# Preparing causal attention inside the stages before it: a four-stage transformer kernel on one Trainium2 core

## The chip, the core and the metric

The kernel runs on one core of a Trainium2 chip. TensorE (PE) multiplies matrices, VectorE (DVE) and ScalarE (ACT) work element by element, GpSimd (POOL) does some adds and powers, and SyncE (SP) issues most DMA transfers. Each engine runs its own instructions in program order; semaphores order them against each other. The metric is the device time in microseconds (us) of one execution.

## The reference, cut to what matters

Two layers over 2 x 2048 tokens of 128 features; each sub-layer f is applied as `x = x + layernorm(f(layernorm(x)))`. The four sub-layers are local attention over segments of 64 tokens, an attention with a mixture of 8 experts and a shared one behind it, causal attention with 2 heads of width 128 and one shared key and value head, and a second, sparse mixture. The change lies in the second and the third:

```python
# second: the mixture; combine holds two non-zero weights a token
shared = _swiglu(xf, sW1, sW2, sW3)
h = silu(einsum('td,efd->etf', xf, eW1)) * einsum('td,efd->etf', xf, eW3)
moe_out = shared + einsum('te,etd->td', combine, einsum('etf,edf->etd', h, eW2))
# third: causal attention, here on layernorm(x)
k = apply_rope(x @ Wk.T); v = x @ Wv.T
q = apply_rope(einsum('btd,hkd->bhtk', x, Wq))
scores = where(causal, einsum('bhtk,bsk->bhts', q, k) * scale, -inf)
out = einsum('bhts,bsk->bhtk', softmax(scores), v).transpose(0, 2, 1, 3).reshape(B, T, 256) @ Wo.T
```

`layernorm` takes off the mean of each token's 128 features and divides by the root of variance plus 1e-5.

## The kernel before

X stays in SBUF as 32 tiles of 128 tokens x 128 features; four tiles are a block of 512 tokens. Products that need precision are split in a high and a low part and made in three matmuls (`matmul_split`, L64 to L66). An `nc.Block()` gives each engine its own list of work; at its end all engines meet.

**The mixture** (`ffn_mixture`, second block) runs over 72 items: 8 token blocks, each with the shared expert and 8 others. For item t TensorE makes the two up products (three items ahead of the down product), ACT the silu (L1624), VectorE the product with the gate side (`hidden`, L1662), GpSimd the expert's weight (L1647), ACT the high part (`high`, L1608), VectorE the low part (`low`, L1667), and TensorE the down product. When a token block's nine items are through, ACT copies the sum (`keep_down`, L1614), TensorE turns it, and `finish` on VectorE takes it in parts, one beside each of the following items, 15 items late (`FIN_LAG`): part 0 adds x2 (L1675), parts 1 to 4 take the statistics of one tile each (L1791, L1793), GpSimd makes the power at part 4 (L1812), parts 6 to 8 apply mean and scale to four tiles (L1683, `APPLY0`), and at part 8 GpSimd adds the result to X (L1639).

**Between** stands a block of its own at the head of `causal_attention`: SP loads the projection weights, the mask and the rotation table `cs` (2 MB, into `room`); VectorE takes the statistics of all 32 tiles in four chunks (L719 to L727), with GpSimd's powers (L738), then rotates the weights (L2051, L2052); ACT makes their high part (L2067), VectorE the low part (L2054). GpSimd zeroes two areas (L2652, L2763).

**Causal attention** runs over two batches. `load(b)` makes the 2048 tokens' keys, queries and values in four turns of 512: VectorE norms four tiles (`norm`, L2223; two turns ahead), TensorE turns them (L2459), ACT makes two copies (`copies`, L2391 and L2392), VectorE the low part (`low`, L2228), TensorE v (L2470) and three rotated projections. For each of the three, VectorE multiplies by `cs` (`rope`, L2235), GpSimd adds the two halves (L2352), ACT makes the high part (L2396), VectorE the low part (L2241). Then 16 rows of 128 queries follow: scores, maxima on VectorE (L2268), exponentials on ACT (L2421), transposes, copies of them on VectorE (L2332), values (L2529), the output copy on ACT (L2429) and `row_done` on VectorE. In batch 1 a function `between` puts work for the last stage beside the rows, among it rows' norms on ACT (L2784). GpSimd's list in a batch is the rotation adds and then one power for each four rows. SP's list holds the last stage's tables and the clearing of d_xs, 17 MB in DRAM.

Of the kernel before, what the change touches and what calls it, by code (L numbers as in the profile page):

```python
# [5 lines left out]
F32 = mybir.dt.float32  # L6
F32R = mybir.dt.float32r
# [6 lines left out]
P = 128  # L14
# [716 lines left out]

def stats_pool(nc, pool, S, rows=slice(0, 2), chunks=range(4)):
# [609 lines left out]
APPLY0 = {6: (0, 1), 7: (2,), 8: (3,)}  # L1342
# [4 lines left out]
def ffn_mixture(nc, dr, X, g, S, w, ao, x2):  # L1347

    m = Mem(nc, "b2_")
    with m:  # L1350
# [190 lines left out]
        F = FinishNorm(m, by_rows=True)  # L1541
        ub = m.ps("ub", 4)
# [35 lines left out]
        with nc.Block() as block:  # L1578
            @block.sync
            def _(sp):  # L1580
# [3 lines left out]

                keep_gates(0)
                for n in range(NBLK):
# [6 lines left out]
                    if n + 1 < NBLK:  # L1593
                        keep_gates(n + 1)

            @block.scalar
            def _(act):
# [21 lines left out]
                for t in range(ITEMS + KEEP_LAG):  # L1619
# [8 lines left out]
                    if k == 0 and n >= 1:  # L1628
                        keep_down(n - 1)
                    n, k = divmod(t, NX)  # L1630
                    if k == TURN_AT + UP_LAG and n + 1 < NBLK:
                        gate_rows(n + 1)

            @block.gpsimd
            def _(pool):
# [5 lines left out]
                for t in range(ITEMS + FIN_LAG):  # L1641
# [10 lines left out]
                    if k == ADD_PART and 0 <= n < NBLK:  # L1652
                        add_back(n)

            @block.vector
            def _(dve):
# [13 lines left out]
                def finish(n, part):  # L1670
# [16 lines left out]
                router.best(nc, dve, 1)  # L1687
                for t in range(ITEMS + FIN_LAG + NX):
# [207 lines left out]
def ffn_layer0(nc, dr, X, g):  # L1896
    with Mem(nc, "b_") as m:
# [12 lines left out]
        ffn_mixture(nc, dr, X, g, S, w, ao, x2)  # L1910
# [95 lines left out]
HC = 2  # L2006
SCALE_C = float(D) ** -0.5


FRONT_AT = 3  # L2010
SENDS = (14, 17)
def causal_attention(nc, dr, X, g, W, LF):
    with Mem(nc, "c_") as m:
        NW = 2 * (1 + HC)
        wh = m.sb("wh", [P, NW, D], F32R)
        wl = m.sb("wl", [P, NW, D], F32R)
        wv = m.sb("wv", [P, D])
        wo = m.sb("wo", [P, HC, D])
        mask = m.sb("mask", [P, P], BF16)
# [7 lines left out]
        with Mem(nc, "c0_") as t:  # L2027
            S = Stats(m, t, g)
            raw = t.sb("raw", [P, NW, D])
            w_in = t.sem("w_in")  # L2030
            c_in = t.sem("c_in")
            rot = t.sem("rot")
            hi = t.sem("hi")
            lo = t.sem("lo")
            with nc.Block() as block:
                @block.sync
                def _(sp):
                    sp.dma_start(raw[:, 0::2, :], dr["c_wkq"]).then_inc(w_in, 16)
                    for dst, src in ((wv[:, :], "c_wv"), (wo[:, :, :], "c_wo"), (mask[:, :], "mask1"),
                                     (cs[:, :, :, :], "cs1")):  # L2040
                        sp.dma_start(dst, dr[src]).then_inc(c_in, 16)
                    sp.wait_ge(c_in, 16 * 4)

                @block.vector
                def _(dve):
                    def weights():
                        dve.wait_ge(w_in, 16)
                        for k in range(0, NW, 2):
                            src = raw[:, k, :].rearrange("p (n two) -> p n two", two=2)
                            dst = raw[:, k + 1, :].rearrange("p (n two) -> p n two", two=2)  # L2050
# [1481 lines left out]
```

## Time and profile before

| | us |
|---|---|
| three runs, median (lowest to highest) | 2020.51 (2020.46 to 2022.98) |
| profiled execution | 2022.49 |
| its span | 2020.3 |
| PE, DVE, POOL, ACT busy of the span | 86%, 72%, 51%, 49% |

The span runs from the first instruction to the last; the execution's own time has about 2 us more around it. In a timeline row stand the start and the length in us, engine, line, operation, what is written and read, and the number of instructions merged (x4); in brackets how long the engine had been idle and what ended that. In the windows busy time is given for PE, PEld (weight loads), DVE, ACT and POOL in this order; a busy PE is not PE at its peak. The granted clock is a share of 2.4 GHz.

### The profile page before, as it was taken

The page shows a single profiled execution, that of the slowest core. Times are in us where ns is not written, and L with a number is a line of the kernel's source. Part 1 is how long each engine was busy: PE and PEld are TensorE (multiplying, and loading weights), DVE is VectorE, ACT ScalarE, POOL GpSimd, SP SyncE. Part 2 cuts the span into 40 slices and gives each one's busy share as a digit, 9 for nine tenths or more (in the row PEclk, how much of TensorE's full clock was granted, in tenths as well). Part 3 has the DMA queues.
Part 4 walks back from the last instruction along what each step waited for, and adds up shares of the span by engine and source line. Part 5 has one row for each costly group of instructions (what it writes and reads, how often), then busy time and mean ns, then how long its engine had stood idle before and what let it go on. Part 6 is the DMA issues. An engine that isn't in the chain of part 4 may idle for free. (4 is left out here: it accounts for less than half of the span.)

```text
span 2020.3 us, 37074 instructions
## 1 busy us (share of the span) xinstructions
PE 1730.4 (86%) x13636; PEld 1314.7 (65%) x13636; DVE 1456.8 (72%) x3406; ACT 984.5 (49%) x2221; POOL 1027.2 (51%) x684
## 2 busy tenths in 40 slices
PE   3899999998589999999998899947898689959993
PEld 2677877877445665666665776625786477748782
DVE  5688778778478877877884688877776777863234
ACT  2456555555315676556656455413332263326564
POOL 3466556556307896777865356642000400356554
PEclk9899999999759999999999899968999899979996
DMA  5212112111100000000000133349200000026663
GB/s 167 79 70 83 63 70 82 69 75 69 44 0 1 1 1 1 1 1 1 1 1 1 45 104 95 94 124 232 44 1 0 1 1 1 23 63 201 207 220 113
DMA packets 78467, 124.08 MB, mean 61 GB/s; under 512 B 11824, under 2 KB 43440, under 8 KB 77776
## 3 DMA queue, kind: packets, MB, share of 16 engines
q1 hardware_dynamic: 73744, 112.31, 18.3%
q0 software_dynamic: 4544, 9.41, 1.4%
q8 instruction: 109, 1.79, 0.4%
q14 instruction: 70, 0.57, 0.1%
HBM read 59.19 MB, written 28.94 MB: 44 GB/s over the span
## 5 line engine op out<-in xcount | busy, mean ns | idle before, releaser
L1088 ACT ACTIVATE mb_pt<-mb_stb 128x1024 f32<-128x1024 f32 x256 | 250.5, 1021 | 128.5 <-PE mb_stb L1233 127.2
L938 DVE TENSOR_REDUCE mb_mxp<-mb_p1b 128x1 f32<-128x512 f32 x352 | 231.4, 685 | 44.6 <-PE mb_p1b L1217 40.7
L1138 POOL TENSOR_TENSOR mb_psum<-mb_pt 128x1024 f32<-128x1024 f32 x70 | 166.9, 2386 | 130.4 <-ACT mb_pt L1088 130.1
L1143 POOL TENSOR_TENSOR mb_psum<-mb_psum,mb_pt 128x1024 f32<-128x1024 f32 x84 | 200.5, 2387 | 19.6 <-ACT mb_pt L1088 9.4
L351 DVE TENSOR_TENSOR ma_tr<-ma_pbank,ma_cs 128x512 f32<-128x512 f32 x256 | 161.7, 684 | 64.8 <-PE ma_pbank L66 54.2
L441 POOL TENSOR_TENSOR ma_qt<-ma_tr,ma_swp 128x512 f32<-128x512 f32 x64 | 82.3, 1289 | 160.2 <-DMA ma_swp<-ma_tr 134.5
L2529 PE MATMUL mc_pv<-mc_pt,mc_v 128*128 128x256 f32 x544 | 147.0, 395 | 17.6 <-DVE mc_pt L2332 17.5
L1217 PE MATMUL mb_p1b<-mb_ks,mb_qs 96*128 96x512 f32 x352 | 146.2, 457 | 5.3 <-DVE mb_mxp L938 1.7
L1812 POOL TENSOR_TENSOR mc_frs<-mc_fve,mc_half 128x4 f32<-128x4 f32 x8 | 8.1, 1013 | 272.3 <-DVE mc_fve L1796 272.2
L490 ACT ACTIVATE ma_e<-ma_sbank,ma_mx 128x80 f32<-128x80 f32 x512 | 119.6, 367 | 49.7 <-DVE ma_mx L358 49.7
L1233 PE MATMUL mb_stb<-mb_qs,mb_ks 98*128 98x512 f32 x512 | 142.7, 401 | 0.4 <-ACT mb_pt L1088 0.4
L1647 POOL TENSOR_TENSOR mb_hh<-mb_hh,mb_gb 128x512 f32<-128x512 f32 x64 | 99.2, 1557 | 79.2 <-DVE mb_hh L1662 78.3
L2332 DVE COPY mc_pt<-mc_tb 128x512 f32<-128x512 f32 (+1 forms) x144 | 94.1, 659 | 60.1 <-PE mc_tb L2514 60.0
L1246 PE MATMUL mb_pvb<-mb_pt,mb_v 128*32 128x256 f32 x2048 | 137.0, 385 | 0.0
L938 DVE TENSOR_REDUCE mb_mxp<-mb_misc 128x1 f32<-128x512 f32 x160 | 109.4, 684 | 17.3 <-PE mb_misc L1217 17.3
L2529 PEld LDWEIGHTS mc_pv<-mc_pt,mc_v 128*128 128x128 f32 x544 | 95.8, 194 | 35.7 <-DVE mc_pt L2332 26.7
L1233 PEld LDWEIGHTS mb_stb<-mb_qs,mb_ks 98*128 98x128 f32 x512 | 94.9, 190 | 29.5 <-issue 9.5
L443 POOL TENSOR_TENSOR ma_kt<-ma_tr,ma_swp 128x512 f32<-128x512 f32 x64 | 96.4, 1508 | 22.3 <-DMA ma_swp<-ma_tr 19.2
L1217 PEld LDWEIGHTS mb_p1b<-mb_ks,mb_qs 96*128 96x128 f32 x352 | 65.9, 195 | 63.0 <-DVE mb_mxp L938 45.2
L3172 POOL DMA_INDIRECT d_ret<-md_ys,md_home x78 | 76.8, 984 | 55.6 <-DVE md_ys L3305 39.2
L500 ACT ACTIVATE ma_pt<-ma_fbank 128x512 f32<-128x512 f32 (+1 forms) x160 | 93.2, 584 | 17.6 <-PE ma_fbank L607 17.6
L64 PE MATMUL ma_pbank<-ma_xth,ma_wh 128*128 128x256 f32 x256 | 85.5, 334 | 15.9 <-DVE ma_tr L351 15.9
(420 smaller groups left out, 4795.7 us busy)
## 6 DMA issues: line engine op xcount, KB each, us to landing
ma_swp<-ma_tr SPq DMA_DIRECT2D x256, 128.0 KB, 2.0
md_wslot<-d_weights SPq DMA_DIRECT2D x39, 516.0 KB, 3.6
d_xs<-mw_blank SPq DMA_DIRECT2D x1, 16899.0 KB, 77.3
mb_gb<-b_gates SPq DMA_DIRECT2D x64, 256.0 KB, 3.2
md_xs<-d_xs SPq DMA_DIRECT2D x39, 131.0 KB, 3.3
md_work<-d_ret SPq DMA_DIRECT2D x8, 512.0 KB, 5.5
mg_X<-x SPq DMA_DIRECT2D x4, 512.0 KB, 10.9
ma_cs<-cs SPq DMA_DIRECT2D x1, 2048.0 KB, 9.2
```

The source lines that it names most:

```text
L351: nc.vector.tensor_tensor(tr[:, G % TRS, part, :, :], pbank[:, i % 2, :].rearrange("p (c t) -> p c t", c=2), cs[:, b // 2, part, None, :]. ...
L443: nc.gpsimd.tensor_tensor(kt[:, par(b), 2 * c:2 * c + 2, :, PM:KEYS0], t0.rearrange("p c (a b) -> p c a b", b=SEG), t1.rearrange("p c (a b ...
L490: nc.scalar.activation(e[:, s, slot, :], sbank[:, 2 * j + k // 4, k % 4 * KEYS0:(k % 4 + 1) * KEYS0], ACT.Exp, bias=mx[:, s, slot:slot + 1 ...
L938: nc.vector.tensor_reduce(mxp[:, r // NCH, r % NCH:r % NCH + 1], pass_bank(r), AXX, ALU.max).then_inc(p1_max, 1)
L1088: nc.scalar.activation(pt[:, T % RING, :, :].rearrange("p (b h) q -> p b (h q)", b=2), stb[:, 2 * (i % 2):2 * (i % 2) + 2, :], ACT.Exp, sc ...
L1138: nc.gpsimd.tensor_tensor(total, pt[:, T % RING, :, :], pt[:, (T + 1) % RING, :, :], ALU.add).then_inc(summed, 1)
L1143: nc.gpsimd.tensor_tensor(total, total, pt[:, (T + i) % RING, :, :], ALU.add).then_inc(summed, 1)
L1217: nc.tensor.matmul(pass_bank(r), qs[V % 3][0:QROWS, h, t * P:(t + 1) * P], ks[V // UNITS][0:QROWS, c * BLK:(c + 1) * BLK], start=True, sto ...
L1233: last = nc.tensor.matmul(stb[:, 2 * (i % 2) + hp, :], ks[U // UNITS][:, i * P:(i + 1) * P], qs[U % 3][:, 2 * hp:2 * hp + 2, :].rearrange( ...
L1246: last = nc.tensor.matmul(pvb[h * DK:(h + 1) * DK, 0:UQ], v1[U // UNITS][:, i, :], pt[:, T % RING, h, :], start=(i == 0), stop=(i == KT - ...
L1647: nc.gpsimd.tensor_tensor(hh[:, t % HR, :], hh[:, t % HR, :], gb[:, q % GBR, :], ALU.mult).then_inc(gated, 1)
L2529: last = nc.tensor.matmul(pv[:, 0:HC * P], v[:, t, :], pt[:, K % 2, a * HC * P:(a + 1) * HC * P], start=(t == 0), stop=(t == r))
```

## The change

The block between the mixture and causal attention is dissolved. A class `CausalWeights` holds its results from before the second sub-layer on.

- *Mixture.* SP loads the weights and the mask at its head (`N.load`). At items 18 to 21 VectorE rotates them, ACT makes the high part, VectorE the low part. The norm of each token block is applied by ACT at part 7, as scale and bias; VectorE makes the bias at part 6. VectorE takes the causal statistics of batch 0's four blocks at part 7 of blocks 1 to 4 and folds them at part 8 of blocks 2 and 4; GpSimd makes their powers in blocks 3 and 5.
- *Causal attention.* `cs` comes in four pieces at the head of its only block, each with its semaphore. `norm` is ACT's, by scale and bias. GpSimd zeroes its areas at the head of its list. The statistics of batch 1 are taken and folded beside rows 9 and 10 of batch 0; their powers stand behind batch 0's second power on GpSimd, and `shift` beside row 12.

```diff
 # ffn_mixture
-APPLY0 = {6: (0, 1), 7: (2,), 8: (3,)}
+APPLY_PART = 7
+PREPARE_AT = 18
@@ sync
+                N.load(sp, dr, raw)
                 keep_gates(0)
@@ scalar
+                def apply(n):
+                    act.wait_ge(biased, n + 1)
+                    for s in range(BPT):
+                        nc.scalar.activation(acc[:, n % 2, s, :], acc[:, n % 2, s, :], ACT.Identity, bias=fnb[:, s:s + 1],
+                                             scale=F.rs[:, s:s + 1]).then_inc(normed, 1)
@@ for t in range(ITEMS + FIN_LAG + NX), behind silu, high, keep_down, gate_rows
+                    if t == PREPARE_AT + 2:
+                        N.high(nc, act, raw)
+                    n, part = divmod(t - FIN_LAG, NX)
+                    if part == APPLY_PART and 0 <= n < NBLK:
+                        apply(n)
@@ gpsimd
+                    if k == 2 and n in (3, 5):
+                        stats_pool(nc, pool, N.S, rows=slice(0, 1), chunks=range((n - 3) // 2, (n - 3) // 2 + 1))
@@ vector, finish
-                    elif part in APPLY0:
+                    elif part == APPLY_PART - 1:
                         dve.wait_ge(F.powed, n + 1)
-                        for s in APPLY0[part]:
-                            nc.vector.tensor_scalar(acc[:, n % 2, s, :], acc[:, n % 2, s, :], F.mv[:, s, 0:1], F.rs[:, s:s + 1],
-                                                    ALU.subtract, ALU.mult).then_inc(normed, 1)
+                        if n > 0:
+                            dve.wait_ge(normed, n * BPT)
+                        nc.vector.scalar_tensor_tensor(fnb[:, :], F.mv[:, :, 0], -1.0, F.rs[:, :], ALU.mult,
+                                                       ALU.mult).then_inc(biased, 1)
+                    if part == APPLY_PART and 1 <= n <= NBLK // 2:
+                        dve.wait_ge(residual, n)
+                        stats_rows(nc, X, N.S, n - 1)
+                    if part == APPLY_PART + 1 and n in (2, 4):
+                        stats_fold(nc, dve, N.S, n // 2 - 1)
+                    if part == APPLY_PART and n == 6:
+                        N.shift(nc, dve, 0)
@@ vector, loop over t
+                    if t == PREPARE_AT:
+                        N.rotate(nc, dve, raw)
+                    if t == PREPARE_AT + 3:
+                        N.low(nc, dve, raw)
 # causal_attention: the block of weights and statistics is removed
@@ sync
+                for i in range(BB):
+                    sp.dma_start(cs[:, i, :, :], dr["cs1"][:, i, :, :]).then_inc(cs_in[i], 16)
                 W.tables(sp, dr)
@@ vector: norm and its calls are removed; in rope
+                    if b == 0 and q % R == 0:
+                        dve.wait_ge(cs_in[q // R], 16)
@@ vector, rows
+                            elif STATS_AT <= r < STATS_AT + 2 and s in (2, 3):
+                                stats_rows(nc, X, S, BB + 2 * (r - STATS_AT) + s - 2)
+                            elif STATS_AT <= r < STATS_AT + 2 and s == 4:
+                                stats_fold(nc, dve, S, 2 + r - STATS_AT)
+                            elif r == STATS_AT + 3 and s == 4:
+                                N.shift(nc, dve, 1)
@@ gpsimd
+                W.zero(nc)
+                LF.zero(nc)
...
+                        if b == 0 and i == 1:
+                            stats_pool(nc, pool, S, rows=slice(0, 1), chunks=range(2, 4))
@@ scalar
+                def norm(b, i):
+                    n = b * BB + i
+                    act.wait_ge(N.shifted, b + 1)
+                    if i >= 2:
+                        act.wait_ge(xt_mm, n - 1)
+                    for s in range(BPT):
+                        tile = n * BPT + s
+                        nc.scalar.activation(xn[:, i % 2, s, :], X[:, tile, :], ACT.Identity, bias=N.nbias[:, tile:tile + 1],
+                                             scale=S.r[:, tile:tile + 1]).then_inc(xn_ready, 1)
@@ scalar, load
+                    norm(b, 0)
+                    norm(b, 1)
                     copies(b, 0)
                     copies(b, 1)
                     for i in range(BB):
                         (copy of v)
+                        if i + 2 < BB:
+                            norm(b, i + 2)
                         rope_high(b, R * i)
```

`stats_rows` takes the statistics of four tiles (bn_stats), `stats_fold` makes mean and variance of eight (eight bn_aggr and three small operations); `shift` makes -mean times scale of 16 tiles.

## Rows read from the trace of the kernel before

**Rows 1.** Windows; columns: stretch, length, busy us (instructions) by engine, granted clock, DMA.

```profile
1180.00:1300.00 120.00, 116.12 (x482) 83.24 (x482) 101.59 (x177) 58.35 (x108) 78.59 (x54) 1.00 0.33 98
1324.20:1345.95 21.75, 0.01 (x1) 0.00 (x0) 15.23 (x100) 0.84 (x1) 10.93 (x9) 0.50 0.33 116
1386.10:1555.90 169.80, 159.51 (x876) 131.96 (x876) 125.71 (x335) 58.47 (x177) 3.03 (x3) 0.95 0.25 52
1372.00:1400.00 28.00, 18.59 (x78) 14.37 (x76) 18.50 (x38) 9.61 (x22) 8.17 (x6) 0.76 1.12 230
```

**Rows 2.** Timeline of the gap: start, length, engine, line; last, the page's DMA issues.

```profile
1328.45 1.11 DVE L1683 TENSOR_SCALAR mb_acc<-mb_acc,mb_fmv,mb_frs 128x128 f32<-128x128 f32 x4 [1.13 <-POOL mb_frs L1812]
1329.64 1.26 POOL L1639 TENSOR_TENSOR mg_X<-mg_X,mb_acc 128x512 f32<-128x512 f32 x1 [1.23 <-DVE mb_acc L1683]
1332.26 1.64 DVE L719 BATCH_NORM_STATS2 mc_bst<-mg_X 128x6 f32<-128x128 f32 x8
...
1334.84 1.64 DVE L719 BATCH_NORM_STATS2 mc_bst<-mg_X 128x6 f32<-128x128 f32 x8
...
1345.95 2.14 DVE L2223 TENSOR_SCALAR mw_room<-mg_X,mc_mean,mc_rs 128x128 f32<-128x128 f32 x8
...
ma_cs<-cs SPq DMA_DIRECT2D x1, 2048.0 KB, 9.2
```

**Rows 3.** Timeline of ACT in batch 1's rows.

```profile
1643.39 3.18 ACT L2784 ACTIVATE mw_xr<-mg_X,mw_nbias,mw_rs 128x128 f32<-128x128 f32 x8
```

**Rows 4.** Timeline of the load of batch 0.

```profile
1350.49 0.73 PE L64 MATMUL mc_sb<-mc_xh,mc_wh 128*128 128x512 f32 x1
...
1352.41 1.23 DVE L2235 TENSOR_TENSOR mw_room<-mc_sb,mw_room 128x1024 f32<-128x1024 f32 x1 [2.98 <-PE mc_sb L66]
...
1353.55 2.09 DVE L2223 TENSOR_SCALAR mw_room<-mg_X,mc_mean,mc_rs 128x128 f32<-128x128 f32 x4
...
1360.94 1.21 DVE L2235 TENSOR_TENSOR mw_room<-mc_sb,mw_room 128x1024 f32<-128x1024 f32 x1
...
1370.07 1.21 DVE L2235 TENSOR_TENSOR mw_room<-mc_sb,mw_room 128x1024 f32<-128x1024 f32 x1
...
1377.27 1.23 DVE L2235 TENSOR_TENSOR mw_room<-mc_sb,mw_room 128x1024 f32<-128x1024 f32 x1
```

**Rows 5.** Timeline between the batches.

```profile
1555.49 0.38 ACT L2429 ACTIVATE mc_ot<-mc_pv 128x256 f32<-128x256 f32 x1 [11.99 <-PE mc_pv L2529]
...
1561.96 2.14 DVE L2223 TENSOR_SCALAR mw_room<-mg_X,mc_mean,mc_rs 128x128 f32<-128x128 f32 x8
...
1562.45 2.17 PE L2459 MATMUL mc_tb<-mg_ident,mw_room 128*128 128x128 f32 x8 [5.82 <-DVE mw_room L2223]
...
1566.30 0.47 PE L64 MATMUL mc_sb<-mc_xh,mc_wh 128*128 128x512 f32 x1
```

**Rows 6.** Timeline of the mixture, one block on ACT and VectorE, then two copies.

```profile
1217.78 0.60 ACT L1624 ACTIVATE mb_s<-mb_ub 128x512 f32<-128x512 f32 x1
...
1219.18 1.31 DVE L1683 TENSOR_SCALAR mb_acc<-mb_acc,mb_fmv,mb_frs 128x128 f32<-128x128 f32 x1
...
1220.43 0.63 ACT L1608 ACTIVATE mb_h_hi<-mb_hh 128x512 fp32r<-128x512 f32 x1 [2.06 <-POOL mb_hh L1647]
...
1238.42 0.58 ACT L1614 ACTIVATE mb_dT<-mb_db 128x512 f32<-128x512 f32 x1
...
1260.52 0.58 ACT L1614 ACTIVATE mb_dT<-mb_db 128x512 f32<-128x512 f32 x1
```

**Rows 7.** Timeline of ACT: output copy of row 14, then of rows 14 and 15.

```profile
1543.11 0.39 ACT L2429 ACTIVATE mc_ot<-mc_pv 128x256 f32<-128x256 f32 x1 [2.13 <-PE mc_pv L2529]
...
1775.55 0.39 ACT L2429 ACTIVATE mc_ot<-mc_pv 128x256 f32<-128x256 f32 x1 [2.13 <-PE mc_pv L2529]
...
1789.10 0.39 ACT L2429 ACTIVATE mc_ot<-mc_pv 128x256 f32<-128x256 f32 x1 [13.17 <-PE mc_pv L2529]
```

**Rows 8.** Groups by line between 1100 and 1700 us: count, busy us, mean ns.

```profile
L2421 ACT ACT_TABLE_LOAD x1 | 1.3, 1283 | 0.0
```

More of the change, by code:

```diff
@@ L729, in stats_vector, with stats_start, stats_rows, stats_fold @@
         mid()
+def stats_start(nc, S):
+    nc.vector.memset(S.half[:, :], -0.5).then_inc(S.step, 1)
+def stats_rows(nc, X, S, n):
+    for i in range(n * BPT, (n + 1) * BPT):
+        nc.vector.bn_stats(S.bst[:, i, :], X[:, i, :]).then_inc(S.step, 1)
+def stats_fold(nc, dve, S, c):
+    at = 1 + c * S.chunk_steps
+    tiles = slice(c * S.CT, (c + 1) * S.CT)
+    for i in range(tiles.start, tiles.stop):
+        dve.wait_ge(S.step, at + i - tiles.start + 1)
+        nc.vector.bn_aggr(S.mean[:, i, :], S.bst[:, i, :]).then_inc(S.step, 1)
+    dve.wait_ge(S.step, at + 2 * S.CT)
+    nc.vector.tensor_scalar(S.vt[:, tiles], S.mean[:, tiles, 1], 1e-5, 1e-5, ALU.add, ALU.mult).then_inc(S.step, 1)
+    nc.vector.tensor_scalar(S.ve[:, 0, tiles], S.mean[:, tiles, 1], 1e-5, None, ALU.add).then_inc(S.step, 1)
+    dve.wait_ge(S.step, at + 2 * S.CT + 2)
+    nc.vector.tensor_tensor(S.ve[:, 1, tiles], S.vt[:, tiles], S.mean[:, tiles, 1], ALU.add).then_inc(S.step, 1)
 def stats_pool(nc, pool, S, rows=slice(0, 2), chunks=range(4)):
@@ L1618, in _ @@
                 router.weights(nc, act, 1)
-                for t in range(ITEMS + KEEP_LAG):
+                def apply(n):
[3 more added lines that the diff above has]
+                                             scale=F.rs[:, s:s + 1]).then_inc(normed, 1)
+                for t in range(ITEMS + FIN_LAG + NX):
                     if t < ITEMS:
@@ L1627, in _ @@
                     n, k = divmod(t - KEEP_LAG + 1, NX)
[L1628 removed]
+                    if k == 0 and 1 <= n <= NBLK:
                         keep_down(n - 1)
@@ L2000, in _, with causal_attention @@
                         nc.scalar.activation(dst[0], raw, ACT.Copy).then_inc(hi, 1)
-HC = 2
-SCALE_C = float(D) ** -0.5
 FRONT_AT = 3
+STATS_AT = 9
 SENDS = (14, 17)
-def causal_attention(nc, dr, X, g, W, LF):
+def causal_attention(nc, dr, X, g, W, LF, N):
     with Mem(nc, "c_") as m:
[L2014 to L2019, printed above, removed]
+        wh, wl, wv, wo, mask, S = N.wh, N.wl, N.wv, N.wo, N.mask, N.S
+        cs_in = [m.sem(f"cs_in{i}") for i in range(BB)]
         room = W.room
@@ L2026, in causal_attention @@
         rp = room[:, at[4]:at[5]].rearrange("p (i c) -> p i c", c=BLK)
[L2027 to L2050, printed above, removed]
-                            nc.vector.tensor_scalar(dst[:, :, 0], src[:, :, 1], -1.0, None, ALU.mult).then_inc(rot, 1)
-                            nc.vector.tensor_copy(dst[:, :, 1], src[:, :, 0]).then_inc(rot, 1)
-                        dve.wait_ge(hi, 1)
-                        nc.vector.tensor_tensor(wl[:, :, :], raw[:, :, :], wh[:, :, :].bitcast(F32),
-                                                ALU.subtract).then_inc(lo, 1)
-                    stats_vector(nc, dve, X, S, 1e-5, weights)
-                @block.gpsimd
-                def _(pool):
-                    W.zero(nc)
-                    LF.zero(nc)
-                    stats_pool(nc, pool, S, rows=slice(0, 1))
-                @block.scalar
-                def _(act):
-                    act.wait_ge(rot, NW)
-                    nc.scalar.activation(wh[:, :, :], raw[:, :, :], ACT.Copy).then_inc(hi, 1)
         xh = m.sb("xh", [P, 2, BLK], F32R)
@@ L2215, in between @@
                         LF.variances(nc, dve, 3)
-                def norm(b, i):
-                    n = b * BB + i
-                    if i >= 2:
-                        dve.wait_ge(xt_mm, n - 1)
-                    for s in range(BPT):
-                        tile = bass.ds(n * BPT + s, 1)
-                        nc.vector.tensor_scalar(xn[:, i % 2, s, :], X[:, tile, :], S.mean[:, tile, 0], S.r[:, tile],
-                                                ALU.subtract, ALU.mult).then_inc(xn_ready, 1)
                 def low(b, i):
@@ L2244, in load @@
                 def load(b):
-                    norm(b, 0)
-                    norm(b, 1)
                     low(b, 0)
```

58 lines of the change are left out of this document (51 added, 7 removed).

## The prediction

> **What bounds the kernel now.** I read the page first (busy shares, then the chain of waits). The chain that ended last lies wholly in the last stage, which the change doesn't touch, so I asked each stage where it starts and what its engines wait for. The windows [rows 1] give four different answers. In a steady part of the mixture TensorE is busy 116 of 120 us: only what makes it wait counts there. Between the mixture and the causal load it is idle for all of 21.75 us. In batch 0's sixteen score rows it is busy 159.5 of 169.8 us. The fourth window, 28 us around the end of the causal load, has 18.6 busy at a mean granted clock of 0.76. The change acts on exactly these four places.
>
> The timeline of the gap [rows 2] shows a serial string: the mixture's last add starts on GpSimd at 1329.64 for 1.26 us; at 1332.26 VectorE starts four chunks of statistics, 2.58 us apart; the causal block's first norm starts at 1345.95. No other engine has work there that the next stage could use.
>
> **The change part by part.**
>
> *The block goes.* Its start (1332.26) is where the causal block can now start (1345.95), both by VectorE's first operation [rows 2]: -13.7 us, its end barrier and the wait for the rotation table among them. That table now comes in four pieces at the head of the causal block; SP issues them before the other tables and the clearing of d_xs. The first use was at 1352.41, 6.5 us after the block's start [rows 2, 4], and needs a quarter of the table. A table of this size, whole, lands in 9.2 us in the first stage [rows 2], so I cost the first quarter at nothing; if it took as long as the whole, it would be 2.7 us late, and that is the bound. The two memsets on GpSimd move to the same block's start, under the same 6.5 us.
>
> *End of the mixture.* The last block's norm was four VectorE operations, 1.11 us [rows 2]; it is now one small product on VectorE and four ACT operations, which take half of the 3.18 us of eight of the same form in the last front [rows 3], 1.6: +0.5, with +0.4 for the extra operation and hand-over. Take +0.9 (bounds 0.4 and 1.5).
>
> *Start of batch 0's load.* VectorE made eight norms in 2.14 us, and ACT's first copy needed only the first four, so it was not behind all of them. Now ACT itself makes eight, 3.18 us [rows 3], before that copy: the copy waits about 3.2 instead of 1.7 us, and with it the low part and the first projection, which came 4.5 us after the block's start [rows 2, 4]. +1.5 (bounds 0.5 and 3).
>
> *The rest of both loads.* A load has four turns of three rotary products. VectorE's first product of each turn starts at 1352.41, 1360.94, 1370.07 and 1377.27 [rows 4]: turns of 8.53 and 9.13 us with four norms in them, and 7.20 without. The norms take 2.09 us there because one of them sits behind GpSimd's add. Without them 1.3 + 1.9 = 3.2 us go, if nothing is late next. On ACT four norms are 1.6 us, put behind the copy of v, where ACT waits for GpSimd's add anyway; at the second turn it just fits. Batch 1's turns have the same norms. I take 3.0 for each load: -6.0 (bounds 0 and -6.5). The upper bound is that ACT's chain of add, high part, low part becomes the limit.
>
> *Between the batches.* After the last row's output copy on ACT (1555.49) TensorE does one small projection and is idle 5.82 us; VectorE meanwhile finishes row 15, waits for GpSimd's power, applies four rows, and only at 1561.96 starts batch 1's norms; the first projection follows at 1566.30 [rows 5]. ACT is free from 1555.9: its eight norms end near 1559.1, the transposes and copies by 1560.3. Then the low part waits only for VectorE's own rows, until 1561.9; plus 0.7 it is ready at 1562.6. So -3.7 (bounds -1 and -4.5).
>
> *Statistics of batch 1 in rows 9 and 10 of batch 0.* Two chunks, 2 x 2.58 = 5.2 us of VectorE [rows 2]. The nearest price is batch 1's last row, where a half chunk is made: 13.55 us from output copy to output copy, against 12.38 in batch 0 [rows 5, 7], so 1.17 us for 1.3 of work. At that rate two chunks cost 4.7. These rows have waits on VectorE's side too, so I take +3.5 (bounds 0 and 5).
>
> *The mixture.* Blocks follow each other at 22.10 us by the copy of the down product [rows 6]. Per block four norms leave VectorE; two of the four take 1.31 us there instead of 0.3, because GpSimd is in an operation of its own [rows 6]. ACT takes 1.6 us instead. In the steady block ACT's silu at 1217.78 ends at 1218.4 and it then waits 2.06 us for GpSimd until 1220.43 [rows 6]. The new burst stands just ahead of that silu and fits into the wait. I choose, from the order of these rows: the hidden product of the next item can run about 0.35 us earlier, GpSimd's gate with it, and the add to X no longer waits 0.2 for the norms; everything behind them in that block comes 0.55 to 0.6 earlier. Seven blocks: -4. Against this: statistics of batch 0's rows in blocks 1 to 4 (stats beside ACT's burst: nothing; two folds, each a chunk's 2.58 less its eight stats' 1.64 [rows 2], 0.9 us: +0.6), two powers on GpSimd in the chain of gates (+1; they were hidden within a chunk's 2.58, which is the upper end for each), six small rotations, one high and one low part of the weights at items 18 to 21 (+1.4). Net -1 (bounds -6 and +5).
>
> Here a page speaks against the change. In the rows two norms of each block take 1.31 us while GpSimd works, and one of the four in a load's turn does so too. The Trainium skill, SBUF - State Buffer, section "Who interferes with whom", says that copies, tensor_scalar and two-input operations with both inputs in SBUF share a port pair with GpSimd by an exclusive lock. By it the rotations, the low part of the weights and the product for the bias, all new in the mixture, would each stand behind a gate; the trace agrees for the norms, and no row shows the new ones. With one gate's length for each group the mixture's net would be about +3 instead of -1.
>
> Sum: -13.7 + 0.9 + 1.5 - 6.0 - 3.7 + 3.5 - 1.0 = -18.5 us. The profiled execution took 2022.49 us, span 2020.3 and 2.2 around it; this becomes a span near 2001.8. The runs' median is 2.0 below the profiled one, so for the median 2020.5 - 18.5 = 2002.0 us.
>
> **The rivals.**
> - *Little besides the block.* ACT becomes the limit in the loads (0 instead of -6) and the rows and the mixture pay their upper bounds: gains of 6 to 15 us, near 2009. For it: ACT's burst in the second turn of a load has no room left; the row loop is 94% busy on TensorE [rows 1]. Against: VectorE is the engine TensorE waits for in all these rows.
> - *More than forecast.* The mixture's stalls all came from the norms, and the clock recovers sooner after shorter idle times (at 0.76 around the load's end [rows 1]): 24 to 29 us, near 1994.
> - *The activation table.* If Identity were not in the set that Silu uses, each of eight blocks would load a table twice, 1.28 us each [rows 8]: +20.5, less some 3 of ACT's wait: near 2019, no change. For it: no row has Identity beside Silu. Against: ACT's Identity operations stand between exponentials in the whole of batch 1 [rows 3], and that stage loads its table once [rows 8]. The Trainium skill, ScalarE: Activation LUTs, section "Table sets: the hidden batching unit", says that identity stands in every set as filler; by it this rival gives nothing at all.
> - *Slower: the clock in the mixture.* It is granted 1.00 over 120 us [rows 1]. Around the load's end, after waits of several us, the mean is 0.76 over 28 us [rows 1], which is about 6.7 us lost. If ACT's burst made TensorE wait long enough in each block for the clock to fall to its lower level (1.2 instead of 2.4 GHz) the same way, each block would pay up to 6.7 us: from three blocks on the gain of 18.5 is gone, with five of eight it is 2035. Against: the burst is 1.6 us long and stands in a wait of ACT's; TensorE never waits more than about 1 us there.
>
> **How the numbers follow.** Forecast (gain 15 to 24): 0.62. Little besides: 0.22. More: 0.10. Table: 0.02. Clock: 0.04. 2002.0 is the forecast's own value. The range 1994 to 2010 leaves out the last two, a part of the second and the far end of the third. About 0.2% (4 us) is what can be told from no change: faster 0.94, same 0.02, slower 0.04.
>
> **What would show it.** VectorE's (now ACT's) first norm some 2.6 us after the mixture's last add, and 1.5 us more to the first projection. Turns of the load near 7.3 us, all four. The idle time of TensorE between the batches 3.7 us shorter to the first projection. Blocks of the mixture near 21.5 us without statistics and above 22 with them. Rows 9 and 10 longer by 1.5 to 2 us each. The prediction is wrong if the blocks of the mixture lengthen beyond 22.7, if the second turn of a load stays at 9, or if a table is loaded between silus.

## The result and the profile after

The changed kernel is faster, by a little under 1%: 2004.98 us in the median of four runs (2002.32 to 2007.5) against 2021.74 for the kernel before on the same chip (2020.46 to 2023.07), a ratio of 0.9913, 95% interval 0.990 to 0.9926. Forecast were 2002.0 us, range 1994 to 2010. The medians lie 16.8 us apart, the two profiled executions 19.8 in span (2020.3 and 2000.5).

Where the span went, stage by stage. Each stage runs from one start to another that both traces have, and the differences add up to the 19.8 but for rounding:

| stage | before | after | difference | predicted |
|---|---|---|---|---|
| span's start to the mixture's first gate copy (unchanged code) | 1140.54 | 1136.58 | -4.0 | 0 |
| to the last copy of a down product in the mixture | 181.91 | 182.04 | +0.1 | -1.0 |
| to the first causal norm (last norm, end, the old block) | 23.50 | 10.15 | -13.35 | -12.8 |
| to the first projection of batch 0 | 4.54 | 5.93 | +1.4 | +1.5 |
| to the first score of batch 0 | 35.67 | 34.48 | -1.2 | -3.0 |
| rows of batch 0, to row 15's output copy | 169.3 | 171.0 | +1.7 | +3.5 |
| to the first projection of batch 1 | 10.81 | 7.22 | -3.6 | -3.7 |
| to the first score of batch 1 | 40.82 | 38.71 | -2.1 | -3.0 |
| rows of batch 1, to row 12's output copy | 136.36 | 138.77 | +2.4 | 0 |
| to the end | 276.87 | 275.62 | -1.2 | 0 |

The timeline of the changed kernel at the gap (start, length, engine, line, operation, count; in brackets the idle time before it and what ended that) answers to [rows 2]:

```profile
1324.27 0.16 DVE L1725 SCALAR_TENSOR_TENSOR mb_fnb<-mb_fmv,mb_frs 128x4 f32<-128x4 f32 x1 [1.12 <-POOL mb_frs L1866]
1324.47 1.65 ACT L1650 ACTIVATE mb_acc<-mb_acc,mb_fnb,mb_frs 128x128 f32<-128x128 f32 x4 [2.70 <-DVE mb_fnb L1725]
1326.19 1.26 POOL L1678 TENSOR_TENSOR mg_X<-mg_X,mb_acc 128x512 f32<-128x512 f32 x1 [1.96 <-ACT mb_acc L1650]
...
1328.77 3.20 ACT L2453 ACTIVATE mw_room<-mg_X,mg_cnbias,mg_rs 128x128 f32<-128x128 f32 x8 [2.65 <-PEq L40]
...
1334.70 0.77 PE L64 MATMUL mc_sb<-mc_xh,mg_cwh 128*128 128x512 f32 x1
...
1337.59 1.22 DVE L2286 TENSOR_TENSOR mw_room<-mc_sb,mw_room 128x1024 f32<-128x1024 f32 x1 [3.94 <-PE mc_sb L66]
```

From the mixture's last add (1326.19) the first causal norm comes 2.58 us later; before, it was 16.31 [rows 2]. The string of statistics is gone, and nothing stands in its place but ACT's eight norms, 3.20 us instead of VectorE's 2.14 [rows 2]. The four pieces of the rotation table land in 6.1 us in the median, issued at 1328.75; the first rotary product starts at 1337.59 and waits for TensorE's product alone.

Between the batches (same view) it answers to [rows 5]:

```profile
1540.17 0.38 ACT L2500 ACTIVATE mc_ot<-mc_pv 128x256 f32<-128x256 f32 x1 [12.00 <-PE mc_pv L2600]
1540.46 3.17 ACT L2453 ACTIVATE mw_room<-mg_X,mg_cnbias,mg_rs 128x128 f32<-128x128 f32 x8
...
1542.26 1.76 PE L2530 MATMUL mc_tb<-mg_ident,mw_room 128*128 128x128 f32 x8 [0.93 <-DVE mc_acc L2345]
...
1546.32 0.29 DVE L1862 TENSOR_TENSOR mg_X<-mg_X,mc_acc 128x128 f32<-128x128 f32 x1
...
1546.64 0.69 DVE L2277 TENSOR_TENSOR mc_xl<-mc_tb,mc_xh 128x512 fp32r<-128x512 f32 x1
1547.39 0.50 PE L64 MATMUL mc_sb<-mc_xh,mg_cwh 128*128 128x512 f32 x1 [1.59 <-DVE mc_xl L2277]
```

ACT norms batch 1 right behind its output copy, and the transposes run while VectorE still applies row 15. What ends last is VectorE's own last row (1546.32) and the low part behind it, as foreseen: 7.2 us from copy to projection, where it was 10.8.

In the mixture two blocks by the copies of the down product, and ACT's part at the head of the first, answer to [rows 6]:

```profile
1214.86 0.58 ACT L1642 ACTIVATE mb_dT<-mb_db 128x512 f32<-128x512 f32 x1
...
1215.81 0.63 ACT L1636 ACTIVATE mb_h_hi<-mb_hh 128x512 fp32r<-128x512 f32 x1
1216.33 1.65 ACT L1650 ACTIVATE mb_acc<-mb_acc,mb_fnb,mb_frs 128x128 f32<-128x128 f32 x4
1217.87 0.58 ACT L1658 ACTIVATE mb_s<-mb_ub 128x512 f32<-128x512 f32 x1
1218.55 0.63 ACT L1636 ACTIVATE mb_h_hi<-mb_hh 128x512 fp32r<-128x512 f32 x1
...
1236.36 0.58 ACT L1642 ACTIVATE mb_dT<-mb_db 128x512 f32<-128x512 f32 x1
1258.52 0.58 ACT L1642 ACTIVATE mb_dT<-mb_db 128x512 f32<-128x512 f32 x1
```

The burst stands ahead of the silu, and no table is loaded around it. The first block, which has four tiles of statistics in it but no fold and no power, takes 21.50 us; the next, with statistics, a fold and a power, 22.16; before, each took 22.10.

Three windows of the changed kernel, then the two of the kernel before at the same distance from the first score of batch 1 as the second and third (stretch, length, busy us and instructions of PE, PEld, DVE, ACT, POOL, then granted clock, DMA share, GB/s); the first answers to [rows 1]:

```profile
1180.00:1300.00 120.00, 114.58 (x483) 83.79 (x482) 96.66 (x208) 67.32 (x131) 81.96 (x56) 1.00 0.31 96
...
1586.00:1600.00 14.00, 11.91 (x50) 9.39 (x51) 7.92 (x33) 5.41 (x18) 4.30 (x2) 0.62 0.00 1
1628.00:1642.00 14.00, 12.84 (x63) 10.77 (x62) 8.17 (x29) 6.59 (x18) 1.64 (x1) 0.77 0.00 0
...
1607.00:1621.00 14.00, 11.05 (x55) 8.56 (x56) 8.90 (x37) 5.47 (x18) 4.32 (x2) 0.76 0.00 1
1649.00:1663.00 14.00, 12.47 (x70) 10.46 (x69) 9.60 (x32) 7.21 (x19) 1.64 (x1) 0.91 0.00 0
```

The clock stayed at 1.00 in the mixture, so the slower rival did not come. VectorE has 5 us less to do there and ACT 9 more. The other windows are in rows of batch 1, where the code is unchanged: rows 1, 2, 5 and 6 there are 0.8, 0.4, 0.3 and 0.9 us longer than before, the rows from 8 on as long as before. The granted clock is lower in the same stretches (0.62 against 0.76, 0.77 against 0.91), so the +2.4 in the table goes with the clock. All twelve traces of kernels with the change show it (138.7 to 139.1 us), against a single trace of the kernel before, so whether the change sets it is open.

### The profile page after: what moved, and what is told of

Same layout as the page of the kernel before. It is cut to its first block and busy times, and to the rows that moved or that the text cites. A ratio compares the mean times of both kernels' runs of the same rounds, so it can differ in the third digit from the quotient of the medians.

```text
span 2000.5 us, 37076 instructions
## 1 busy us (share of the span) xinstructions
PE 1727.7 (86%) x13636; PEld 1312.6 (66%) x13636; DVE 1426.2 (71%) x3352; ACT 1008.7 (50%) x2285; POOL 1026.4 (51%) x684
## 3 DMA queue, kind: packets, MB, share of 16 engines
q8 instruction: 109, 1.79, 0.4%
## 5 line engine op out<-in xcount | busy, mean ns | idle before, releaser
L1866 POOL TENSOR_TENSOR mc_frs<-mc_fve,mg_half 128x4 f32<-128x4 f32 x8 | 8.1, 1013 | 244.5 <-DVE mc_fve L1850 244.5
```

## The experiments

The first two groups, of four kernels each, ran on two other chips, where every kernel, the one before too, takes some 50 us longer, about 28 of them in one row of the traces (last section); so there only ratios and stage lengths are compared. Kernels of one group are compared with the same runs of the kernel before. Every change of a total below is under 1%; what an experiment decides is read from its stages. The table's stages of the kernel before come from one trace, on the first chip.

**First group: the two norms, each put back on VectorE.** e1:

```diff
 # mixture, vector
-  product for the bias at part 6; ACT: apply(n) at part 7
+  tensor_scalar(acc, mean, rs) of tiles 0, 1 at part 6, tile 2 at part 7, tile 3 at part 8
```

> The changed kernel with the mixture's norm back on VectorE (four tensor_scalar at parts 6, 7 and 8), all else as changed. Theory A (moving the norm to ACT gains about 0.6 us in each block, the folds and powers of the moved statistics give it back): blocks without fold or power, 21.5 us in the changed kernel, go back to 22.1; blocks with a fold and a power, 22.15, go to 22.7 or more, since the statistics' operations now stand beside the norms; the mixture 4 to 6 us longer, the end of the mixture 0.3 shorter, the whole near 2008 to 2010. Rival B (ACT's norm gains nothing, the shorter blocks come from something else, as the weights and statistics being made early): blocks stay within 0.2 us of 21.5 and 22.15, the whole near 2004 to 2005.

Measured: 2064.11 us, ratio 0.996 (0.9948 to 0.9973). The mixture took 189.5 us, 7.5 more than in the profiled changed kernel. The blocks were 23.21, 22.78, 24.09, 22.78, 23.73 from the second on, where the changed kernel has 22.44, 21.50, 22.16, 21.47, 22.15. The timeline of e1 around one block with statistics shows why more than the 4 us of the forecast came back:

```profile
1217.16 0.59 DVE L1712 TENSOR_SCALAR mb_acc<-mb_acc,mb_fmv,mb_frs 128x128 f32<-128x128 f32 x2
...
1218.88 1.31 DVE L1712 TENSOR_SCALAR mb_acc<-mb_acc,mb_fmv,mb_frs 128x128 f32<-128x128 f32 x1
1220.11 0.86 DVE L738 BATCH_NORM_STATS2 mg_bst<-mg_X 128x6 f32<-128x128 f32 x4
...
1218.43 1.67 POOL L1684 TENSOR_TENSOR mb_hh<-mb_hh,mb_gb 128x512 f32<-128x512 f32 x1 [1.74 <-DVE mb_hh L1701]
1221.64 1.68 POOL L1684 TENSOR_TENSOR mb_hh<-mb_hh,mb_gb 128x512 f32<-128x512 f32 x1 [1.53 <-DVE mb_hh L1701]
```

The third norm falls into GpSimd's gate (1.31 us), the statistics stand behind it, and the next gate starts 3.21 us after the first. In the changed kernel that distance is 2.49 with the same statistics; in the kernel before, with the norms but no statistics, it is 2.43. So four tiles of statistics cost 0.66 us a block with the norm on VectorE (22.78 against 22.12 before) and nothing with it on ACT (21.50, against 21.48 in the second block of e10 below, which has neither statistics nor weights in it). The expectation's theory A holds, and more than it said came back. The move to ACT pays for the change's other additions, besides its own gain.

e2:

```diff
 # causal attention
-  ACT: norm(b, 0), norm(b, 1) ahead of its copies, norm(b, i + 2) behind the copy of v
+  VectorE: norm(b, 0), norm(b, 1) ahead of low(b, 0), norm(b, i + 2) behind rope and rope_low
```

> The changed kernel with the causal load's norms back on VectorE (eight ahead, then two turns ahead), all else as changed. Theory A (ACT's norms gave 3.6 us between the batches, 1.6 and 0.5 in the first two turns of each load and cost 1.4 at the first start): batch 0 starts its first projection 4.5 us after the block's start instead of 5.9; turns of 8.5 and 9.1 in place of 6.9 and 8.6; output copy of row 15 to first projection 10.8 instead of 7.2; the whole 3.6 + 2 x 2.1 - 1.4 = 6.4 us longer, near 2011. Rival B (the gain between the batches comes from TensorE's lists being shorter or from the clock): row 15 to first projection stays under 8, the whole within 2 us of the changed kernel's.

Measured: 2064.4 us, ratio 0.9957 (0.9942 to 0.9972); theory A holds in the stages. The first projection came 4.91 us after the first norm (5.93 with ACT), the loads took 35.53 and 41.57 us, the stretch between the batches 11.02 (7.22). The gain between the batches is all from ACT's norms (3.8), and their price at the start is 1.0.

**e3: places of the second fold and of the powers.**

```diff
-  fold at part 8 of blocks 2 and 4; powers at k == 2 of blocks 3 and 5
+  fold at part 8 of block 2 and at part 3 of block 5; powers at (4, 2) and (6, 6)
```

> The changed kernel with the fold of the second chunk at part 3 of block 5 instead of part 8 of block 4, and the powers at other places: the first at part 2 of block 4 instead of block 3, the second at part 6 of block 6 instead of part 2 of block 5. Changed kernel, by the copy of the down product: blocks 25.10, 22.44, 21.50, 22.16, 21.47, 22.15. Theory A (a power of 1.64 us on GpSimd in the chain of gates costs the 0.6, the fold nothing): the 0.6 follows the powers: to the block that holds item 53 (power 1) and the one that holds item 75 (behind the last item: free), so one of the two long blocks becomes 21.5. Rival B (the fold costs it): the first long block stays at its place, the second moves to where the fold is. The whole 0 to 1 us shorter.

Measured: 2058.55 us, ratio 0.9942 (0.9919 to 0.9964). The block with a power and no fold takes 21.49, like one with neither: a power among the gates costs nothing, and theory B holds. A fold costs 0.65 at part 8 and 1.0 at part 3. The second power, now behind the last item, was not free: the `shift` on VectorE waits for it (until 1321.98), the last block's copies and statistics stand behind that, and the stretch from the last copy of a down product to the first causal norm was 11.70 us, where the other traces of changed kernels have 9.8 to 10.6. The changed kernel's VectorE and GpSimd at a fold:

```profile
1241.32 0.63 DVE L746 BATCH_NORM_AGGREGATE mg_mean<-mg_bst 128x2 f32<-128x6 f32 x8
1241.99 0.60 DVE L748 TENSOR_SCALAR mg_vt<-mg_mean 128x8 f32<-128x8 f32 x1
1242.50 0.16 DVE L749 TENSOR_SCALAR mg_ve<-mg_mean 128x8 f32<-128x8 f32 x1
1242.69 1.15 DVE L751 TENSOR_TENSOR mg_ve<-mg_vt,mg_mean 128x8 f32<-128x8 f32 x1
...
1240.82 1.74 POOL L1686 TENSOR_TENSOR mb_hh<-mb_hh,mb_gb 128x512 f32<-128x512 f32 x1 [0.80 <-DVE mb_hh L1703]
1242.52 1.30 POOL L1678 TENSOR_TENSOR mg_X<-mg_X,mb_acc 128x512 f32<-128x512 f32 x1
```

Two operations on 8 columns take 0.60 and 1.15 here, against 0.17 each in the fold of batch 0's rows (1452.79), where GpSimd is idle: each ends as GpSimd's operation does (1242.56, 1243.82). The statistics reading of 8 tiles just ahead (0.63) is not held up. The lengthening is the lock of the Trainium skill, SBUF - State Buffer, section "Who interferes with whom": the trace agrees for tensor_scalar and for an operation with both inputs in SBUF, however few their columns. The prediction's estimate by that page, +3 for the mixture, was too high all the same, because most additions found GpSimd idle: the rotations took 0.19 us each, the weights' low part 0.95 and the eight products for the bias 0.15 or 0.16.

**e4: the load's second turn.** In the changed kernel it still takes 8.62 us, against 6.89 and 7.19 for its neighbours. Were ACT's norms 3 and 4 in the way?

```diff
-  ACT: norm(0, 0), norm(0, 1); norm(b, i + 2) behind the i-th copy of v
+  ACT: norm(0, 0) alone, VectorE norm(0, 1); norm(b, 2), norm(b, 3) behind the first copy of v
```

> The changed kernel with the causal load's norms placed otherwise: VectorE makes the second four tiles' norm of batch 0 (ACT the first), and ACT makes the third and the fourth four right behind the first copy of v instead of one turn apart. Theory A (in the second turn ACT's norm stands between GpSimd's add and the high part and costs 1.4 us in each load; at the start ACT's second four stand before the first copy and cost 1.4): first projection 4.5 us after the block's start, second turn 7.2 instead of 8.6 in batch 0 and 1.4 shorter in batch 1; the whole 4 us shorter than the changed kernel, near 2001. Rival B (the second turn is long because of GpSimd's locks or the low part's order on VectorE): second turn stays above 8.3, only the 1.4 of the start goes.

Measured: 2056.62 us, ratio 0.9925 (0.9903 to 0.9946). The first projection came 0.86 us sooner, but the second turn stayed at 8.46 with no norm in it. The timeline of e4, second turn, ACT's part left out:

```profile
1348.86 1.21 DVE L2287 TENSOR_TENSOR mw_room<-mc_sb,mw_room 128x1024 f32<-128x1024 f32 x1
...
1350.15 1.29 POOL L2414 TENSOR_TENSOR mw_room<-mw_room 128x512 f32<-128x512 f32 x1 [0.68 <-DVE mw_room L2287]
1350.17 1.82 DVE L2293 TENSOR_TENSOR mc_kql<-mw_room,mc_kqh 128x512 fp32r<-128x512 f32 x1
...
1353.05 0.68 DVE L2293 TENSOR_TENSOR mc_kql<-mw_room,mc_kqh 128x512 fp32r<-128x512 f32 x1
```

GpSimd's add of the rotary halves starts 0.02 us ahead of VectorE's low part, which then takes 1.82 us instead of 0.68. The changed kernel has the same pair at 1351.34 and 1351.35. So theory B: what is left of the long turn goes with this collision, not with ACT's norms. Nor is it new. In the second turn of the kernel before, beside VectorE's norms, stood the same pair:

```profile
1362.08 0.68 DVE L2241 TENSOR_TENSOR mc_kql<-mw_room,mc_kqh 128x512 fp32r<-128x512 f32 x1
...
1368.30 1.30 POOL L2352 TENSOR_TENSOR mw_room<-mw_room 128x512 f32<-128x512 f32 x1 [0.68 <-DVE mw_room L2235]
1368.33 1.82 DVE L2241 TENSOR_TENSOR mc_kql<-mw_room,mc_kqh 128x512 fp32r<-128x512 f32 x1
```

In batch 0's first three turns of all thirteen traces, the turns with such a low part (1.79 us or more) take 8.45 to 9.79 us, the others 6.87 to 7.42, with or without ACT's norms in them. The kernel before had one in both of its turns with norms; the change took it out of the first and left it in the second. What did come new into GpSimd's shadow is the second turn's first low part. It was 0.68 us before (1362.08); now it waits for ACT's high part and lies beside an add:

```profile
1345.78 1.29 POOL L2405 TENSOR_TENSOR mw_room<-mw_room 128x512 f32<-128x512 f32 x1 [0.18 <-DVE mw_room L2286]
1346.30 1.33 DVE L2292 TENSOR_TENSOR mc_kql<-mw_room,mc_kqh 128x512 fp32r<-128x512 f32 x1 [0.59 <-ACT mc_kqh L2463]
```

**Second group: the changed kernel again, and the block alone.** e5 is the changed kernel unaltered.

> The changed kernel itself, beside the three others of this job, as their base. Theory A and rival B alike: about 17 us below the kernel before; blocks of the mixture 25.1, 22.4, 21.5, 22.15, 21.5, 22.15, rows 9 and 10 of batch 0 at 12.9 and 14.1.

Measured: 2055.65 us, ratio 0.9904 (0.9874 to 0.9934). The mixture took 182.7, the loads 35.56 and 40.25 (38.71 in the first trace): the same instructions, 1.5 us apart in the second load.

e6 puts both kinds of norm back on VectorE (e1 and e2 together), so it keeps the dissolved block and the moved work alone.

> The changed kernel with both norms, the mixture's and the causal load's, back on VectorE: what is left is the dissolved block, the moved weights and statistics, the table in four pieces. Theory A (the dissolved block alone gives 13.4 us; moved statistics cost 7 in the mixture while the norms stay on VectorE and 2.9 in the rows; the norms on ACT give 7.5 + 5.5): 12 to 13 us longer than the changed kernel, 4 shorter than the kernel before. Rival B (the moved statistics are cheap and the ACT norms worth little in total): within 6 us of the changed kernel.

Measured: 2069.41 us, ratio 0.9983 (0.9966 to 0.9999): 13.8 us longer than e5, a little over theory A's 12 to 13. The gap was 13.67 us shorter than before, but the mixture 6.7 us longer (blocks of 23.24, 22.78, 24.08, 22.77, 23.74 against 22.1), rows 9 and 10 longer by 2.8, the first projection later by 0.4. The work taken out of a stretch where nothing ran beside it was put into stretches where VectorE sets the pace: by these stages three quarters of what the block gave was paid back, and what the norms on ACT do is to win it again.

**e7: folds in the mixture's tail**, where the last item has gone.

```diff
-  fold at part 8 of blocks 2 and 4, powers in blocks 3 and 5, shift at part 7 of block 6
+  fold and power at part 5 of blocks 6 and 7, shift at part 8 of block 7
```

> The changed kernel with the two folds of batch 0's statistics in the two waits of VectorE for GpSimd's power at the mixture's end (part 5 of blocks 6 and 7, 1.1 us each), their powers behind these, the shift last. Theory A (a fold of about 1.1 us beside the items costs 0.65 us, in the waits nothing): all blocks from the third on 21.5, so 1.3 us less up to the last block, the stretch from the last copy of the down product to the causal block's start as before within 0.3; the whole 1.3 shorter. Rival B (the folds or powers meet GpSimd's own power there and lengthen the end): the end 1 us or more longer, the whole the same.

Measured: 2055.75 us, ratio 0.9915 (0.9891 to 0.994). All blocks from the third on, to the last whole one, took 21.48 to 21.50 and the end stayed at 10.52 (10.49 in e5): the folds' 1.3 us are gone, as theory A had it, while the medians differ by nothing that can be told.

**e8: the statistics of batch 1 one tile at a time** over rows 8 to 11 of batch 0.

```diff
-  rows 9, 10: four tiles at slots 2 and 3, fold at slot 4
+  from row 8 on: bn_stats of tile j and bn_aggr of tile j-1 in each slot, 10 slots a chunk; shift one row later
```

> The changed kernel with the statistics of batch 1 spread over twenty slots of rows 8 to 11 of batch 0, one tile's stats and one tile's aggregate in each, instead of bursts of four and eight in rows 9 and 10. In the changed kernel the two rows are 1.3 and 1.6 us longer than before. Theory A (a burst delays VectorE's copy of transposed weights, for which TensorE waits; a single tile's 0.3 us fits into VectorE's waits): rows 8 to 11 together 0.5 us or less longer than in the kernel before, so 2.4 shorter than in the changed kernel. Rival B (the rows are bound by the sum of VectorE's work): rows 8 to 11 together 2.5 to 3.5 us longer than before, no gain.

Measured: 2057.3 us, ratio 0.9919 (0.9893 to 0.9946). Rows 8 to 11 took 10.92, 12.16, 13.00, 14.17 us, against 10.61, 12.85, 14.07, 13.85 in e5 and 10.63, 11.57, 12.50, 13.85 before: 1.7 us more than before, where the bunched form costs 2.8, so between the two theories. It saves 1.1; spread work is not free in a row loop whose TensorE is busy 94% [rows 1].

**Third group, on a chip where the kernel before takes 2020.69 us.** e10 rotates and splits the weights at the head of the mixture's second block rather than at items 18 to 21.

```diff
+  rotate behind router.shifted, high behind router.probabilities, low behind stats_start
-  rotate, high, low at items 18, 20, 21
```

> The changed kernel with the causal weights made at the head of the mixture's second block instead of at items 18 to 21: rotations on VectorE before the router's second half, the high part on ACT between the router's two exponentials, the low part on VectorE before the first hidden product, where VectorE and ACT wait for each other and for a table (2.3 and 2.4 us). Theory A (the weights cost 0.6 us in the first block and 0.9 in the second, since their operations stand between VectorE's parts of the items): blocks 24.5 and 21.5 instead of 25.1 and 22.4, the stretch up to the first copy of the down product at most 0.5 longer, net 1.0 to 1.6 us shorter. Rival B (the first two blocks are longer because ACT's norm of block 0 and the router's finds meet): blocks unchanged at 25.1 and 22.4, the start up to 1 us longer.

Measured: 2007.59 us, ratio 0.9939 (0.9914 to 0.9963). The first two intervals fell from 25.10 and 22.44 to 24.49 and 21.48, so the weights cost 1.6 at items 18 to 21. But the first copy of a down product came 33.54 us after the gates instead of 30.74. TensorE, GpSimd and VectorE in e10 at the head:

```profile
1144.41 0.80 PE L64 MATMUL mb_ub<-mb_nh,mb_w 128*128 128x512 f32 x1 [4.41 <-DVE mb_hh L1702]
1145.03 1.27 POOL L1685 TENSOR_TENSOR mb_hh<-mb_hh,mb_gb 128x512 f32<-128x512 f32 x1 [23.52 <-DVE mb_hh L1702]
1145.05 1.80 DVE L1707 TENSOR_TENSOR mb_h_lo<-mb_hh,mb_h_hi 128x512 fp32r<-128x512 f32 x1
1145.85 0.63 PE L64 MATMUL mb_ub<-mb_nh,mb_w 128*128 128x512 f32 x1
```

The first hidden product comes 7.76 us after the first gate copy instead of 5.43, since the weights' operations stand ahead of it; that is 2.3 of the 2.8. Behind it TensorE has waited 4.41 us and makes 10 matmuls at about 0.63 us, where the granted clock is 0.50, instead of 0.39; in the profiled changed kernel it waits 2.07 us and makes 7 so. The low part meets GpSimd's gate (1.80). Work set at a stage's head delayed the whole pipe behind it by more than it cost inside, and more than either theory had.

e11 joins e4, e7, e8 and e10.

> All found so far together: weights at the head of the mixture, folds in its tail, statistics of batch 1 spread over rows 8 to 11, the second norm of batch 0 on VectorE and the third and fourth right behind the first copy of v. Theory A (the savings add up since they lie at separate places): 1.5 + 1.3 + 1.2 + 0.9 = 4.9 us below the changed kernel, mixture 178.5 to 179 us from the first gate copy to the last down copy. Rival B (what is saved before a load is lost in it, by the phase of GpSimd's adds and the clock): the mixture shorter as said, the whole less than 2 us below the changed kernel.

Measured: 2003.45 us, ratio 0.9917 (0.990 to 0.9933). e12 is the changed kernel beside it.

> The changed kernel itself as the base of this job, with more rounds: ratio to the kernel before 0.990 to 0.993 by either theory.

Measured: 2004.53 us, ratio 0.9917 (0.9899 to 0.9935). The combination saved 1.3 (folds), 1.1 (rows), 0.85 (start) and 1.6 (weights) where foreseen and gave back 3 at the mixture's head, so that the mixture took 182.2 us instead of the expected 178.5 to 179; against the changed kernel (1.1 us by the medians) no difference can be told, where 4.9 were expected. The obvious next version, e11 without e10, was not run.

## Why the prediction was right

*Block and end: right.* -13.7 and +0.9 foreseen, -13.7 and +0.4 measured (+0.7 in e5 and e12); e6 has the same 13.7 without ACT's norms.

*Start of batch 0's load: right.* +1.4 against +1.5; 1.0 of it is ACT's norms (e2), the rest was there without them.

*Between the batches: right to 0.1*, by the mechanism named: 3.8 of e2.

*Rows 9 and 10: a little high.* +2.85 against +3.5, the bunch costing 55% of the 5.2 us of work. The table shows +1.7 for all rows because others ran 1.2 shorter (row 1 4.78 us instead of 6.16).

*The mixture: net right, two terms off.* The norms gave 0.63 us in each of the six blocks that have one in them (-3.8; foreseen -4 over seven). The folds cost 1.3 instead of 0.6, by the lock; the powers nothing instead of 1; the weights 1.6 instead of 1.4. That makes -0.9, and e2 and e4 have mixtures of 181.1 us against 181.9 before. The profiled one shows +0.1 because its first copy came 30.7 us after the gates, as in e1, e3, e5 and e12 (30.6 to 30.7), where the kernel before and e2, e4, e6, e7 and e8 have 29.2 with the same work there, and because its last block was 0.7 shorter than in most. The 1.5 us at the head go with the clock: over the 14 us behind the first gate copy it is 0.77 or 0.78 in the first set and 0.92 or 0.93 in the second, with 14 or 15 up matmuls at its lower level's length instead of 5 or 6. Why it falls once more in some executions is open.

*The rest of the loads: the step that failed.* It said "-6.0 (bounds 0 and -6.5)" from turns near 7.3 us. The trace shows -3.3. Over the eight traces with the loads' norms on ACT as the change puts them (the profiled one, e1, e3, e5, e7, e8, e10, e12) the loads averaged 35.2 and 39.1 us, over the three without (before, e2, e6) 35.6 and 41.3: -2.6 in all, and for batch 0 almost nothing. I read the difference between the turns with norms and the one without as the norms' price. That difference also held something else: in both turns with norms (1359.21 and 1368.33) a low part took 1.8 us beside GpSimd's add, in the turn without norms none did (e4's rows above). In the first turn it went away with the norms, and the turn fell to 6.89 us, below the 7.2 foreseen. In the second it stayed, another low part was lengthened to 1.33 us, and turn 2 went from 9.13 only to 8.62. Batch 1's turns were 8.5, 11.7 and 9.7 us before and are 6.9, 11.2 and 9.7, so "near 7.3, all four" was never to be had there. In batch 0, besides, the clock stayed at its lower level (granted 0.50, 1.2 GHz) for the first 2.5 us of the projections, against 0.89 before: six matmuls took 0.57 to 0.77 us, and the first rotary product came 2.9 us behind the first projection instead of 1.9 [rows 4]. In e2, e4 and e6, where the first projection comes up to 1 us sooner, none or one is slow and the distance is 1.7 or 1.8. The named sign of being wrong, a second turn that stays at 9, came in two of the eight traces (9.54 in e7 and 9.79 in e8, with the changed kernel's code in the loads).

*The total came out closer than its terms, in part by luck.* The change's own terms, with the averages above and the end as in e5 and e12, are -13.0 + 1.4 - 3.6 + 2.85 - 0.9 - 2.6 = -15.9 us. The medians of the kernels themselves lie 16.8, 16.2 (e5) and 16.2 us (e12) below the kernel before on their chips. The profiled pair shows 19.8, and 4 us of it fell ahead of the mixture in unchanged code. The first gate copy lies between 1135.9 and 1140.5 us in all thirteen traces, whatever the kernel; in the changed kernel alone at 1136.6, 1138.99 and 1139.4. The sum leaves out two differences in unchanged code, this one and the +2.4 in batch 1's rows: with one trace of the kernel before, neither can be put to the change or taken from it. So -18.5 was some 2.5 us too much: the loads' 3.4 short, the rows' and the end's 0.9 the other way. Of the rivals, "little besides the block" was half right on the loads. "More than forecast" (24 to 29) is out by every median. The activation table and the falling clock are excluded by the mixture's rows above.

## What to carry to other kernels

Work moved out of an idle stretch into a busy one is worth the stretch less what it delays there: price it by the engine that sets the pace in the new place, and move something off that engine in the same change. A tensor_scalar or a two-input operation of VectorE with its inputs in SBUF can be counted at its own length only where GpSimd is idle (the statistics here were not held up). Before the difference between two stretches is put down to the operations that are to move, look which others in the longer one stand beside GpSimd too: they may stay when these are gone. Stages with waits in them vary by 1 to 3 us between traces of the same code (34.1 to 36.1 us for batch 0's load), so a gain of that size must be read from the same stage in several traces, and not from the total.

## What the runs showed that was not expected

*ScalarE's norm* of a 128x128 tile with scale and bias read per partition: four in 1.64 us, eight in 3.20, in every stage.

*A stall of VectorE's copies on two of the chips.* In all eight traces of the first two groups row 13 of batch 1 took 43.6 to 45.5 us instead of 15.6. No trace of the kernel before was taken there, but its runs are some 50 us longer too. From the timeline of e4, VectorE and TensorE, and two of GpSimd's indirect issues:

```profile
1737.72 0.60 PE L2600 MATMUL mc_tb<-mg_ident,mw_room 128*128 128x128 f32 x4
...
1747.22 0.96 POOL L3031 DMA_INDIRECT d_xs<-mw_xr,mw_posu  x1 [0.30 <-issue]
1748.07 0.69 DVE L2388 COPY mc_pt<-mc_tb 128x512 f32<-128x512 f32 x1 [7.58 <-remote]
1748.48 0.96 POOL L3031 DMA_INDIRECT d_xs<-mw_xr,mw_posu  x1 [0.30 <-issue]
1748.82 2.08 PE L2615 MATMUL mc_pv<-mc_pt,mc_v 128*128 128x256 f32 x4 [10.50 <-DVE mc_pt L2388]
1750.69 1.06 PE L2600 MATMUL mc_tb<-mg_ident,mw_room 128*128 128x128 f32 x4
...
1762.18 0.69 DVE L2388 COPY mc_pt<-mc_tb 128x512 f32<-128x512 f32 x1 [13.42 <-issue]
```

The two copies start 9.8 and 10.4 us after TensorE has made their input (its rows end at 1738.32 and 1751.75), with VectorE idle for 7.58 and 13.42 us before them, while GpSimd issues an indirect transfer every 1.27 us. On the chip of the profiled pair GpSimd issues at the same pace (1727.49, 1728.75, 1730.02 in the changed kernel), and VectorE's copies beside it are not held up. So the issues alone don't cause it; what does is open.
